# Gated MLP of a two-layer transformer: statistics one step ahead of the normalisation, rotation tables scaled in later steps

## What is computed

```python
def _layer(x, wqkv, qs, ksc, wo, lg, lb, w1, b1, w2, b2):
    h = shift_token(x)
    q, k, v = split(h @ wqkv)                 # 8 heads of 64
    q, k = rotary_xpos(l2norm(q) * qs, l2norm(k) * ksc)
    x = x + local_attention(q, k, v) @ wo     # windows of 64
    h = shift_token(x)
    mu = h.mean(-1, keepdims=True)
    var = h.var(-1, keepdims=True)
    h = (h - mu) / jnp.sqrt(var + 1e-05) * lg + lb
    a, g = split(h @ w1 + b1)                 # 341 values each
    h = a * gelu(g)
    return x + h @ w2 + b2
```

## Time and profile before

| | us |
|---|---|
| runs of the kernel before | 1182.98, 1184.93, 1184.94 |
| median | 1184.93 |
| the profiled execution | 1182.32 |
| its span in the profile | 1180.5 |
| attention of layer 0 ends, MLP body begins | about 491 |
| MLP of layer 0 ends | about 566 |
| attention of layer 1 ends, MLP body begins | about 840 |
| MLP of layer 1 ends | about 910 |

### The profile page before, as it was taken

How to read it: one execution, slowest core, us unless ns; L and a number is a source line. 1 busy time by engine, 2 the same in 40 slices (tenths; PEclk the granted TensorE clock), 3 DMA queues, 4 the chain that set the end, 5 groups by cost and what they waited for, 6 DMA issues and landing times. The chain is left out here.

```text
span 1180.5 us, 33825 instructions
## 1 busy us (share of the span) xinstructions
PE 1060.1 (90%) x11683; PEld 729.0 (62%) x11683; DVE 899.6 (76%) x2972; ACT 850.7 (72%) x2674; POOL 660.2 (56%) x1070
## 2 busy tenths in 40 slices
PE   6689996599999999789799999998899799999996
PEld 4466674267777776556477777776566488853442
DVE  4799998478888888565588888887475655289998
ACT  2678884488988898423589888987345766478886
POOL 1578985688888888200588888887133400002222
PEclk9899998799999999899899999999799999999999
DMA  7000000021321211131112222122000343200000
GB/s 237 3 2 10 11 3 1 16 49 38 71 54 47 50 45 47 39 120 34 40 38 47 47 47 47 38 47 47 21 1 20 85 112 86 49 6 17 17 19 18
DMA packets 66498, 50.86 MB, mean 43 GB/s; under 512 B 42262, under 2 KB 53442, under 8 KB 66050
## 3 DMA queue, kind: packets, MB, share of 16 engines
q1 hardware_dynamic: 66339, 48.84, 16.3%
HBM read 21.41 MB, written 2.38 MB: 20 GB/s over the span
## 5 line engine op out<-in xcount | busy, mean ns | idle before, releaser
L1168 PE MATMUL psum<-wa_wqkv,wa_hT 128*128 128x512 f32 x384 | 190.9, 606 | 4.4 <-DVE wa_tmp L1032 3.2
L1124 ACT ACTIVATE wa_p<-psum,wa_nb 128x128 f32<-128x128 f32 x512 | 184.2, 399 | 4.3 <-DVE wa_nb L1048 4.2
L1048 DVE CUSTOM_DVE_ANT_0 psum<-psum,wa_bias 128x128 f32<-128x128 f32 x512 | 133.0, 323 | 51.4 <-PE psum L1197 51.4
L1014 POOL TENSOR_TENSOR wa_p<-wa_p,wa_rrs 128x512 f32<-128x512 f32 x128 | 133.3, 1041 | 49.1 <-DVE wa_rrs L1057 49.1
L1709 POOL TENSOR_TENSOR ex_total<-ex_total,mod 128x128 f32<-128x128 f32 x32 | 15.5, 485 | 211.3 <-DVE ex_total L1837 211.3
L1124 ACT ACTIVATION_READ_ACCUMULATOR wa_p<-psum,wa_nb 128x1 f32 x512 | 122.7, 240 | 0.0
L1884 ACT ACTIVATE cv_z_ex_yw<-psum,ex_w 128x128 f32<-128x128 f32 x384 | 107.0, 401 | 20.1 <-DVE ex_w L1813 7.7
L1955 PE MATMUL psum<-ex_wc,ex_hT 128*128 128x512 f32 x256 | 117.9, 603 | 3.4 <-DVE cv_z_ex_yw L1820 2.1
L985 POOL TENSOR_TENSOR wa_qr<-wa_qr,wa_tmp 128x512 f32<-128x512 f32 x64 | 81.9, 1280 | 64.3 <-DVE wa_tmp L1032 64.3
L1134 ACT ACTIVATE wa_pT<-psum 128x512 f32<-128x512 f32 x128 | 76.6, 598 | 40.2 <-PE psum L1177 40.2
L1177 PE MATMUL psum<-ident,wa_p 128*128 128x128 f32 x512 | 81.4, 283 | 10.1 <-ACT wa_kT L1117 3.2
(11 more groups left out here) (258 smaller groups left out, 3007.2 us busy)
## 6 DMA issues: line engine op xcount, KB each, us to landing
wa_vm<-wa_v SPq DMA_DIRECT2D x127, 128.0 KB, 2.3
cv_toep<-cv_zpad SPq DMA_DIRECT2D x32, 136.0 KB, 2.7
cv_toep<-cv_zpad SPq DMA_DIRECT2D x16, 264.0 KB, 4.2
wa_tabs<-in_rotations_dram SPq DMA_DIRECT2D x2, 2048.0 KB, 8.0
wa_rows<-y_rows SPq DMA_DIRECT2D x31, 128.0 KB
wa_rows<-y_rows SPq DMA_DIRECT2D x31, 127.0 KB
x_rows<-in_L_attn_x_dram SPq DMA_DIRECT2D x4, 512.0 KB, 5.8
out_dram<-x_rows SPq DMA_DIRECT2D x32, 64.0 KB, 1.5
```

What stands on the lines that cost most here:

```text
L1014: nc.gpsimd.tensor_tensor(p, p, cols_bc(rrs[:, t % 2, r, :], P), ALU.mult)\
L1048: m = nc.vector.tensor_tensor_reduce(out=s, in0=s, in1=edges, scale=-1.0, scalar=MAX_FLOAT, op0=ALU.add, op1=ALU.min, accum_out=nb[:, t % ...
L1124: e = nc.scalar.activation(pr[:, t % 2, r, h, :], sim_bank[r][:, P * h:P * h + P], ACT.Exp, bias=nb[:, t % 2, r, h:h + 1], scale=-1.0, acc ...
L1168: nc.tensor.matmul(bank, hT[:, t % 3, :], wqkv[:, INNER * k:INNER * k + INNER], start=True, stop=True).then_inc(done.sem, 1)
```

## The change

In the MLP every function but `statistics` and POOL's `inverse_std` gets one more step of lag, so that these two run one step ahead of `normalize`. A phase now has 13 steps. The timetable puts MLP step 0 two attention steps earlier, so that the old steps 0 and 1 are now steps 1 and 2 at the same places. `statistics` waits in addition for `v_hn` of group g − 2, since `ml_mv` has two buffers. The four scalings of the tables move from steps 4 to 7 (of 12) to steps 7 to 10 (of 13). The ACT table loads and the work for the next block keep their places.

```diff
@@ gpsimd(gp) of gated_mlp
-            return Phase(conv_rows(gp, conv.inverse_std, 5) + [(inverse_std, 0)] +
-                         ([] if more else [(conv_gated, 4)]), first, GROUPS)
+            return Phase(conv_rows(gp, conv.inverse_std, 6) + [(inverse_std, 0)] +
+                         ([] if more else [(conv_gated, 5)]), first, GROUPS)
@@ vector(dve)
             def statistics(g):
+                v_hn.wait(dve, g - 2)
                 for i in range(GT):
...
-            return Phase([(residual, 4)] + conv_rows(dve, conv.statistics, 5) +
-                         [(statistics, 0), (multiply, 2), (normalize, 0)] + conv_rows(dve, conv.offsets, 5), first, GROUPS,
-                         between={4 + k: tables(k) for k in range(4)} if more else None,
+            return Phase([(residual, 5)] + conv_rows(dve, conv.statistics, 6) +
+                         [(statistics, 0), (multiply, 3), (normalize, 1)] + conv_rows(dve, conv.offsets, 6), first, GROUPS,
+                         between={7 + k: tables(k) for k in range(4)} if more else None,
                          begin=lambda: wait_layer(dve, l))
@@ scalar(act)
-            return Phase([(gelu, 2), (hn_columns, 1)] + conv_rows(act, conv.normalized, 5), first, GROUPS,
+            return Phase([(gelu, 3), (hn_columns, 2)] + conv_rows(act, conv.normalized, 6), first, GROUPS,
@@ tensor(pe)
-            return Phase([(up, 2), (turn, 1), (down, 3)], first, GROUPS, begin=lambda: wait_layer(pe, l),
-                         between=None if more else {11: conv_weights})
+            return Phase([(up, 3), (turn, 2), (down, 4)], first, GROUPS, begin=lambda: wait_layer(pe, l),
+                         between=None if more else {12: conv_weights})
@@ layers_in_one_block
-    ATT, MLP = TILES + 5, GROUPS + 4
+    ATT, MLP = TILES + 5, GROUPS + 5
...
-        steps.insert(len(steps) - 3, (m, 0))
-        steps.insert(len(steps) - 1, (m, 1))
-        steps += [(m, s) for s in range(2, MLP)]
+        steps.insert(len(steps) - 5, (m, 0))
+        steps.insert(len(steps) - 3, (m, 1))
+        steps.insert(len(steps) - 1, (m, 2))
+        steps += [(m, s) for s in range(3, MLP)]
```

More of the change, by code:

```diff
@@ L1488, in gelu @@
                                          bias=b1[0:w, 1, k:k + 1]).then_inc(a_gelu[k].sem, 1)
-            between = {2: lambda: nc.scalar.preload_act_table_set("gelu_and_others")}
+            between = {3: lambda: nc.scalar.preload_act_table_set("gelu_and_others")}
             if not more:
-                between[10] = lambda: nc.scalar.preload_act_table_set("natural_log_exp_and_others")
-                between[11] = lambda: conv.copy_weights(act, turn_bank)
-            return Phase([(gelu, 2), (hn_columns, 1)] + conv_rows(act, conv.normalized, 5), first, GROUPS,
+                between[11] = lambda: nc.scalar.preload_act_table_set("natural_log_exp_and_others")
+                between[12] = lambda: conv.copy_weights(act, turn_bank)
+            return Phase([(gelu, 3), (hn_columns, 2)] + conv_rows(act, conv.normalized, 6), first, GROUPS,
                          between=between,
```

## The result

| kernel | median | runs | ratio to before, with its 95% interval |
|---|---|---|---|
| before | 1183.95 | 1182.57 to 1184.94 (4) | |
| changed | 1167.03 | 1163.94 to 1171.24 (4) | 0.9853, 0.9828 to 0.9879 |

The changed kernel is 16.9 us faster. The forecast was 1169.0 us, with a range from 1162.5 to 1177. Its profiled execution took 1171.24 us, 11.1 less than the profiled one of before. It is the slowest of the four, so the two traces show less than the medians do, and part of what follows is about where the rest went.

A forecast was written before the change was run, and what follows sets the result against it. The prediction took TensorE, busy for 90% of the span, to bound the kernel. Its terms −5.4 − 5.9 + 1.8 + 2.2 − 6.0 = −13.3, from the profiled 1182.32 us, gave 1169.0 us, range 1162.5 to 1177.

The forecast's parts named there:

- tables: Layer 0's MLP: scaling later ends DVE's wait for weights, PE's 3.66 us gap and a slow `down`: −5.4 us.
- waits at the entries: End of each attention phase: DVE no longer waits for POOL before four normalisations: −5.9 us.
- new first step: Between attention steps 31 and 32: group 0's POOL operations delay `scale_q`, so PE waits 0.9 us a layer: +1.8 us.
- shared port: At both entries: POOL's power beside DVE's normalisation slows it by 0.54 us, four times: +2.2 us, bounds 0 and 1.04 each.
- clock: Four half-clock stretches after PE's entry gaps cost at most 10.2 us; 6 taken as regained: −6.0 us.
- rival 3: Only the tables' stall goes; entries stay late through ScalarE's exponentials and POOL's scaling of `p`: −3.6, 1178.7 us, chance 6%.
- Rival 1: Each of four entry normalisations is blocked for POOL's whole power: +4.2 instead of +2.2, 1171.0 us, chance 12%.
- rival 2: The full clock doesn't come back at the entries: −7.3 in all, 1175.0 us, chance 20%.
- Rival 4: Slower: the entries' half clock stays and five new half-clock stretches of 1.70 us arise elsewhere: 1185 us or more, chance 3%.

The follow-up runs named there:

- the second comparison: The unedited changed kernel run again beside two edited variants, taking turns on one chip: median 1164.55 us, ratio 0.9868; the kernel before took 1181.83 us there.
- gaps filled: Kernel before, plus 20 unused transposes in each of PE's two gaps ahead of the late outputs of either layer: 1178.01 us, ratio 0.9966.
- the run again: The changed kernel without any edit, measured and profiled once more: median 1164.55 us, ratio 0.9868, profiled span 1159.5 us.
- The wide multiplication: Changed kernel, plus an unused POOL multiplication of 512 elements a partition ahead of the inverse deviation of groups 1 and 2 in each layer: 1172.83 us.

## Why the prediction came out right

The total was right (1167.03 in a range from 1162.5 to 1177, and 2 us from the forecast), the parts less so. The sum of the local terms was too small by 5 us: by the measured ones it would have been 1182.32 − 18.3 = 1164.0. The changed kernel's median came out at 1164.55 in the second comparison and at 1167.03 in the first, which holds more of the half clock in untouched code. So the forecast was nearer to the first median than its terms deserve. That nearness is luck: the port and the clock were both mis-sized in the direction of too small a gain, and untouched code happened to take much of the difference back.

| step | predicted | measured | by |
|---|---|---|---|
| tables | −5.4 | −5.5 | tables alone, 22.07 to 16.54 |
| waits at the entries | −5.9 | −6.3 | 2 × 2.5 net (gaps filled against changed) + 2 × 0.68 |
| new first step | +1.8 | +1.4 | 2 × 0.68, statistics to statistics |
| shared port | +2.2 | 0 | 1.08 us in all four places |
| clock | −6.0 | −7.8 | gaps filled against before |
| sum (before rounding) | −13.3 | −18.3 | stretches of before and changed |
| untouched stretches | 0 | +7.2 in this pair of profiles | (start +4.2, rest +3.2, between −0.3); against the run again −2.7 in all |

- **Tables**: right in size and place. I had put DVE's request at 518 and the landing at 510 to 514. They came at 521.2 and 515.6, in a trace that is 4.2 us later by its start; the margin of 5.7 lies between the 4 and the 8 named. What I missed is that this stall grows when the entry gets faster. Had the entry alone been changed, its forecast would have been 1.9 us too good.
- **Waits**: right. What is measured is above the 5.9 because the idle time in brackets counts from the end of the aggregates: the normalisation started 1.86 us after them before (473.34 to 475.20) and starts 0.30 after them now (478.25 to 478.55), 1.56 sooner, and is 0.03 shorter. DVE's idle time before all four normalisations is gone, PE's gaps are 1.27 and 1.51 for 1.2 and 1.6, and nothing else was as late (rival 3 is out).
- **First step**: right mechanism, 0.70 for the 0.9 us gap. Part was made up in the following step, where PE's wait fell from 0.93 to 0.78.
- **Shared port**: wrong. The nearest row was a POOL multiplication of 512 elements a partition, and I carried its price over to a power of 4. The wide multiplication gave back just such a price, +0.72, by holding one DVE instruction to its end; the power held none. The bound that I put at 0 was the one that held. Rival 1 is out too: DVE's fourth instruction started behind the power and took 0.34 us.
- **Clock**: it came back in both entries (rival 2 is out). The 6 of 10.2 us that I took were 1.8 too few. The step that failed is the share: time at half clock turned into time lost by 76%, not 59%. The count by stretches from the kernel with only the tables moved says about the same: (48.56 − 45.17) + (49.24 − 45.15) = 7.5.
- **Rival 4** is out. The changed kernel's first profile does have half clock further on, at 910 to 915 us (0.50), 970 to 975 (0.66) and 1015 to 1025 (0.85 and 0.81). But the first of these is the same code as 925 to 930 in the profile of before, some 70 us after layer 1's first `down`, where the clock was 0.66, and as 900 to 910 in the changed kernel's second one (0.70 and 0.62). At the other two places neither of those profiles was below 0.9. (Five new stretches of 1.70 us would also have made 1183.5 us and not the 1185 that I named.)

Still open is what decides in which execution the start stays long at half clock; no run here could steer it.

## What to carry to other kernels

When a wait is taken out in front of a load whose landing moves less than the wait was worth, part of it turns up again at the load: make the room at both places in one change. Before you carry the price of an operation beside another engine's over to a different operation, look at the single instructions: which one was held, and until when. And compare profiles stretch by stretch, with one more profile of the same code beside them, before a difference in untouched code is put down to the change.

## What the runs showed of the hardware

- Of the same code, one execution's linear attention runs at clock 0.51 from 50 to 70 us, with PE busy for 19.20 of the 20.00, while another's runs at 1.00, with PE busy for 16.39. The start took 4.8 us longer. A PE that is busy all the time is no sign of full clock: at the lower clock the same work fills the time.
- A POOL power over 128 × 4 elements takes 1.04 us and one multiplication over 128 × 512 takes 1.05, and only the second one slows DVE's normalisation (1.08 to 1.80 us). It does so by holding one of its four instructions: 1.06 us instead of about 0.3, until 0.08 us after the multiplication's end.
- PE's gaps of 1.27 and 1.51 us left the entries at clock 1.00 in both profiles of the changed kernel. Those of 2.00 and 2.23 us, in the run with the wide multiplication, left it in layer 0, and in layer 1 the clock fell. Those of 2.72 and 3.09 us in layer 0 before were both followed by half clock.
- The same load, issued in the same place, landed 53.7 us after r in one run and 55.7 in another (509.32 − 455.60 and 513.37 − 457.70). So a margin of less than 2 us behind this load can be gone in another execution.
